# Second attention layer: the transposed context is copied out of PSUM before the exponentials of the same step instead of after them

## What is computed

```python
lat = layernorm(latents, ln_l_w, ln_l_b)
ctx = layernorm(context, ln_c_w, ln_c_b)
q = (lat @ Wq)        # 16 heads of 64
k, v = jnp.split(ctx @ Wkv, 2, axis=-1)
attn = jnp.einsum('bhnd,bhsd->bhns', q, k) * scale
attn = jnp.clip(attn, -11.0, 11.0)
attn = jax.nn.softmax(attn, axis=-1)
out = jnp.einsum('bhns,bhsd->bhnd', attn, v)
return out @ Wo + bo
```

## Time and profile before

| | |
|---|---|
| median of 3 executions | 2045.55 us (2044.47 to 2047.56) |
| profiled execution, its own time | 2041.5 us |
| its span, first to last instruction | 2039.8 us |
| second attention layer, about | 894 to 1624 us of the span |
| steady part of it, its groups 1 to 13 | 978 to 1530 us |
| PE busy in the steady part | 515.19 of 552 us |

### The profile page before, as it was taken

How to read it: one execution, slowest core, us unless ns; L and a number is a source line. 1 busy time by engine, 2 the same in 40 slices (tenths; PEclk the granted TensorE clock), 3 DMA queues, 4 the chain that set the end, 5 groups by cost and what they waited for, 6 DMA issues and landing times. The chain is left out here.

```text
span 2039.8 us, 47379 instructions
## 1 busy us (share of the span) xinstructions
PE 1799.8 (88%) x16643; PEld 1642.5 (81%) x16643; DVE 1244.3 (61%) x4006; ACT 901.5 (44%) x2276; POOL 601.5 (29%) x731
## 2 busy tenths in 40 slices
PE   6999999999996499967999988989998289999990
PEld 5899999899995488856888877878887289999990
DVE  3567777777777233335777766768776344555545
ACT  4777777777774133323433333423342033333330
POOL 1012232232232200024234333333421254445420
PEclk9999999999998699978999999999998689999996
DMA  6687010011000589972232111111100142222106
GB/s 229 248 273 258 27 42 37 26 39 38 26 30 24 167 284 299 295 240 79 84 110 69 48 43 50 38 46 51 51 25 23 58 158 94 88 79 83 52 33 252
DMA packets 134144, 214.13 MB, mean 105 GB/s; under 512 B 16878, under 2 KB 85009, under 8 KB 133952
## 3 DMA queue, kind: packets, MB, share of 16 engines
q1 hardware_dynamic: 106560, 147.89, 21.6%
q0 software_dynamic: 23040, 59.58, 8.9%
q10 hardware_dynamic: 4352, 4.20, 0.6%
HBM read 111.88 MB, written 103.68 MB: 106 GB/s over the span
## 5 line engine op out<-in xcount | busy, mean ns | idle before, releaser
L467 POOL DMA_INDIRECT buf<-a_rxn,a_disp x192 | 197.0, 1026 | 241.2 <-DVE comb L882 102.8
L621 ACT ACTIVATE a_S<-a_S,a_mn 128x128 f32<-128x128 f32 x512 | 198.9, 395 | 45.5 <-DVE a_mn L912 45.5
L82 PE MATMUL e_psH<-e_x_hi,e_w_hi 128*128 128x256 f32 x640 | 181.9, 284 | 0.0
L83 PE MATMUL e_psH<-e_x_lo,e_w_hi 128*128 128x256 f32 x640 | 178.7, 279 | 0.0
L84 PE MATMUL e_psH<-e_x_hi,e_w_lo 128*128 128x256 f32 x640 | 178.5, 279 | 0.0
L603 ACT ACTIVATE a_kT<-a_psP 128x512 f32<-128x512 f32 x128 | 75.7, 593 | 208.3 <-PE a_psP L84 208.3
L82 PE MATMUL a_psP<-a_c_hi,a_wk_hi 128*128 128x256 f32 x512 | 157.4, 307 | 9.8 <-DVE a_c_lo L774 9.7
L82 PE MATMUL a_psP<-a_x_hi,a_wq_hi 128*128 128x256 f32 x512 | 155.9, 305 | 5.2 <-DVE a_x_lo L774 5.2
L1207 PE MATMUL a_psM<-a_wo,a_oT 128*128 128x256 f32 x512 | 123.7, 397 | 30.6 <-ACT a_plain L564 23.4
L83 PE MATMUL a_psP<-a_c_lo,a_wk_hi 128*128 128x256 f32 x512 | 148.2, 290 | 0.0
L84 PE MATMUL a_psP<-a_c_hi,a_wk_lo 128*128 128x256 f32 x512 | 148.2, 290 | 0.0
(11 more groups left out here) (203 smaller groups left out, 5464.1 us busy)
## 6 DMA issues: line engine op xcount, KB each, us to landing
buf<-a_zeros SPq DMA_DIRECT2D x16, 1320.0 KB, 8.6
buf<-a_zeros SPq DMA_DIRECT2D x16, 1024.0 KB, 6.0
e_rows<-buf SPq DMA_DIRECT2D x64, 256.0 KB, 3.9
e_w_in<-in_L_ffn_w SPq DMA_DIRECT2D x64, 256.0 KB, 3.2
y<-e_y SPq DMA_DIRECT2D x64, 256.0 KB, 3.2
a_ctx<-in_ctx SPq DMA_DIRECT2D x32, 256.0 KB
e_w_out<-in_L_ffn_w SPq DMA_DIRECT2D x64, 128.0 KB, 3.8
y<-a_zeros SPq DMA_DIRECT2D x32, 256.0 KB
```

Source lines behind the costliest of these rows:

```text
L82: pe.matmul(dst, a_hi, b_hi, start=start, stop=False)
L83: pe.matmul(dst, a_hi, b_lo, start=False, stop=False)
L467: g_.indirect_dma_start(out=buf, out_offset=bass.IndirectOffsetOnAxis(ap=disp[:, par, i, k:k + 1], axis=0), in_=rxn[:, par, i], in_offset= ...
L621: ins = a.activation(s[:, h], s[:, h], ACT.Exp, bias=mn[:, u % 2, h:h + 1], scale=-1.0, accum_out=z[:, u % 2, h:h + 1])
```

## The change

```diff
                 if proj:
                     evac_job(plus(g, 1), 1 - par, EARLY[w][0])
+                if not first and prep and w == 3:
+                    evac_ctx(plus(g, 2))
                 exponentials(g, 2 * w)
-                if prep and w == 3:
+                if first and prep and w == 3:
                     evac_ctx(plus(g, 2))
                 if proj:
                     evac_job(plus(g, 1), 1 - par, EARLY[w][1])
```

## The result

| | before | after |
|---|---|---|
| median of the timed executions | 2046.55 us (2044.47 to 2049.99, 4) | 2014.35 us (2012.43 to 2015.19, 4) |
| profiled execution, its own time | 2041.5 us | 2015.19 us |

The ratio of the times is 0.9843, with a 95% interval from 0.9824 to 0.9862: 32.2 us less by the medians, 26.3 us less between the two profiled executions. Repeated later on two chips (e2 and e12) the ratios were 0.9848 and 0.9858. The forecast was 2021 with a range of 2014 to 2030, so the time lies in the range, at its low end; the gain lies above the 20 to 27 us of the forecast itself.

A forecast was written before the change was run, and what follows sets the result against it. PE was taken to set the pace, idle in 12 waits for plain. 23.6 us for waits less ties, plus 1.7 for the clock, minus 1.2 for back edges, gave 24.1 off 2045.55: 2021.4 us, range 2014 to 2030.

The forecast's parts named there:

- What bounds the kernel: Stretch from 978 to 1530 us: PE sets the pace, with 515.19 us of work and waits of 23.4 and 13.4 us.
- The copy goes first: ACT in step 3: evac_ctx starts at about 1214.57, plain is out at about 1215.6, and the exponentials lose nothing.
- The upper end: Output projection in 12 groups: 26.5 us gained without any wait, including 0.10 us a group for shorter matmul rows.
- `oT` tie: PE's output projection: its weight load then waits for DVE's oT, 0.13 us lost per group.
- The `route_shift` tie: PE's transpose_x in the next step: waits for DVE's route_shift about 0.1 us more in each of 12 groups.
- DVE's split of `c_lo`: DVE in step 3: loses its 0.61 us wait, counted as nothing because POOL holds the norms behind it.
- The back edges: PE's three stalls at the loop's jumps: each grows by 0.4 us, 1.2 us lost in all.
- The clock: Output projection behind the wait: one of 12 took 5.41 instead of 3.72 us at a slow clock; 1.7 us gained.
- the clock is worth more: Rival: two or three further slow projections in timed executions are saved too, 28 to 31 us gained, 2017 to 2014.5; chance 0.10.
- DVE next: Rival: oT or route_shift comes some 1 us later than worked out, 12 us of gain lost, 2033 us; chance 0.09.
- nothing: Rival: evac_ctx starts no earlier, or PE's 2 us wait returns whole elsewhere, 2045 us; chance 0.05.
- slower: Rival: the wait returns whole ahead of transpose_x, each with the slow clock, 18.7 us on top, 2064 us; chance 0.02.

The follow-up runs named there:

- e2: The changed kernel, unchanged, measured a second time beside the kernel before: 2017.68 us, ratio to before 0.9848.
- e12: The changed kernel, unchanged, measured a third time on another chip: 2016.91 us, ratio to before 0.9858.
- e6: The kernel before with the move only in the loop's groups, 8 of the 12 that wait: 2028.20 us, ratio to before 0.9917.
- e7: The kernel before with ACT's copies of the transposed context one job later instead of earlier: 2059.11 us, ratio to before 1.0057.
- e8: The changed kernel with DVE's subtraction for c_lo put behind the first normalisation of step 3: 2016.76 us, ratio to before 0.9858.
- e1: The kernel before, unchanged, timed against itself and profiled again: 2049.80 us, ratio to before 1.0006.
- e5: The kernel before with 7 useless PE products inside each of the 12 waits ahead of the output projection: 2035.43 us, ratio to before 0.9938.
- e9: The changed kernel with route_shift ahead of step 0's scores and the c_lo subtraction behind the first normalisation: 2018.57 us, ratio to before 0.9860.
- e10: The changed kernel with PE's second-layer loop, groups 4 to 11, written out and the other engines' loops kept: 2007.52 us, ratio to before 0.9813.

## Why the prediction held, and what was off

**What bounds the kernel**: right. PE's work and two kinds of waits filled the stretch, and a wait taken from PE came through to the end. e6 and e7 show it in both directions, wait by wait.

**The copy goes first**: right. `evac_ctx` starts 0.49 us after job 9's copy; the exponentials lost nothing.

**The upper end and the `oT` tie**: right in place. Of the 26.5 us 1.2 stand for shorter rows, which would show in the steps from 3 to 1. The rest less the tie, 25.3 - 12 x 0.13 = 23.8 us, was forecast for the steps from 1 to 3; 24.75 were measured. The shorter rows came in part only: 0.07 us in each of the four groups out of the loop, 0.3 us in all, and nothing in the loop, where `oT` still holds the weight load.

**The `route_shift` tie**: right in place, too small in size. 0.11 us in each of 12 groups, 1.3 us, had been worked out, which the 1.2 us of shorter rows would have made good. The steps from 3 to 1 lost 2.24 us in nine groups, and at 0.3 for each of the three others 3.1 us. The step that failed is the sentence on DVE's split of `c_lo`, "I count nothing for it": losing its wait put it beside L434, and the norm came 0.21 us later, 0.21 of the 0.28 us that the step of the earlier trace rows lost. e8 shows the contention; that it is the whole of the excess is shown in three groups only, where the step fell by that 0.2 us.

**The back edges**: 1.2 us against the change were forecast, as stalls that grow. The stalls did not (13.4 and 13.2 us). The pair of profiles does lose 1.1 us there beyond the tie, by a slower clock. The stretches behind the second back edge, before and then after:

```profile
1268.00:1270.00 2.00, 1.41 (x14) 1.42 (x16) 1.20 (x3) 0.00 (x0) 0.83 (x1) 0.67 0.47 129
1270.00:1272.00 2.00, 2.00 (x13) 1.78 (x12) 0.69 (x1) 0.00 (x0) 0.00 (x0) 0.50 0.04 10
1272.00:1274.00 2.00, 2.00 (x18) 2.00 (x18) 0.00 (x0) 0.96 (x2) 0.00 (x0) 0.98 0.00 0
```

```profile
1254.00:1256.00 2.00, 1.76 (x16) 1.77 (x16) 1.43 (x3) 0.00 (x0) 1.39 (x3) 0.50 0.40 119
1256.00:1258.00 2.00, 2.00 (x12) 1.78 (x11) 1.97 (x5) 0.00 (x0) 0.87 (x1) 0.50 0.42 121
1258.00:1260.00 2.00, 2.00 (x14) 2.00 (x14) 0.39 (x1) 0.71 (x2) 0.00 (x0) 0.69 0.04 14
```

PE resumes at 1268.59 and at 1254.24 behind stalls of nearly the same length; before, the clock is back after about 3.5 us, after the change it takes about 5. Other executions differ: without the slow projection a back edge step took 24.6 to 26.4 us in e1 and 24.7 to 25.8 in e2 and e12. So the term is no property of the change. The mechanism that I gave for it, taken from one pair of rows, was wrong too: in e1 a slow projection stands ahead of each of the three back edges, and the stalls are 4.60, 4.10 and 5.33 us.

**The clock**: the term that was mis-sized. I put in 1.7 us, one slow projection of 12, because one profile showed one; e1 shows eight, e5 measures 10 us for keeping PE busy. My 24.1 us with 2.0 us less for the waits and ties together (21.6 instead of 23.6), 1.2 more for the back edges and two to five further slow projections (3 to 8 us) would be 27 to 32 us, and 28 to 32 were measured in three comparisons (after, e2, e12); how many such projections a typical execution has, and how much the last groups add, is an estimate from e5, the granted clocks and the two profiles, not a count. The rival "the clock is worth more" had this mechanism, its sign and its place; it had 1 chance in 10, though the 4 us between the profiled execution and the timed ones, for which the forecast had no explanation, spoke for it. The gain of 32.2 us is that rival's and not the forecast's 20 to 27: the time lies in the range because the range had been drawn down to this rival.

**The rivals that fell**: DVE next (PE has no entry for DVE in its list of waits of the steady part), nothing, slower. The last had its price right in kind: e7 shows what a longer wait with the slow clock costs.

## What to carry to other kernels

A short wait of TensorE can cost twice, once as idle time and, in some executions, once more in the work behind it; so count how often the slow form appears over several executions, not in one profile, and compare the granted clock of the timed executions with that of the profiled one before the profile is taken for typical. When a wait is removed, look at what the neighbours do at their new, earlier times: an instruction that "loses its wait" may land on another engine's. And what an engine just behind the bound gains is worth more once the bound moves: the two steps of e9 took 2.65 us off the steady time of the changed kernel, and 6.4 off that of e10.

## What was not expected of the hardware

- Seven useless products in a gap of 2 us made the kernel 10.4 us faster (e5). With them PE's stalls at the back edges also became shorter, 10.5 us for three, and 9.3 with fifteen, instead of 12.7 to 14.3; in e5 no time came of it, since the scores behind them were at the slow clock longer (back edge steps of 24.97 to 25.17 us, before 24.7 to 25.1). Why the number of PE's instructions should shorten the stall stays open.
- The projection in the group right behind a back edge was slow in none of the profiles of before, e1 and e7 (as at 1224.71 and 1311.17 in e1, 1226.24 in e7), the one in the group after that in all three places in e1 and in e7 (as at 1264.24 and 1266.26), and in none in before. Why is open too.
- A jump back costs PE 4.1 to 5.3 us of stall where no fill stands ahead of it, and with the slow clock behind it the step is about 6.5 us longer (e12); DVE's costs 2.6 to 3.4.
